# Rearranging the first prologue of a four-layer transformer kernel on one Trainium2 core

## The chip, the cores and the metric

The kernel is one program on one core of one Trainium2 chip. The metric is the device time of one execution in microseconds (us). A core has five engines that run side by side, each with its own instruction stream: TensorE (PE: matrix products and transposes), VectorE (DVE), ScalarE (ACT), GpSimd (POOL) and SyncE (SP), which here only issues DMAs. ACT and POOL can issue DMAs too. Engines wait for one another through semaphores. A wait stands in an engine's stream, so everything behind it on that engine waits as well.

## The reference

Four residual layers work on `x` of 8 batches x 256 tokens x 512 channels: a rotary cross-attention, a mixture of experts, a second cross-attention, and a layer of routed weight maps. Cut to what this case touches, the first attention and the part of the last layer that is prepared beside it:

```python
# first layer, per batch: 32 heads of 16 channels
q = rope((layernorm(x) @ Wq)); k, v = split(ctx @ Wkv); k = rope(k)
w = softmax(einsum('bqhd,bkhd->bhqk', q, k) / 4)
x = x + tanh(g_xattn[0]) * (einsum('bhqk,bkhd->bqhd', w, v) @ Wout + bout)
...
# last layer: 4096 values added to a 512 x 512 map, for each of 8 experts
deltas = softmax(expert_atom_weights) @ atoms          # (8, 4096)
weighted = deltas * sigmoid(importance)
rows, cols = mask_idx // 512, mask_idx % 512
out = xt @ W.T + segment_sum((xt[:, cols] * vals).T, rows).T
```

The kernel builds the last layer's maps ahead of time: a `table` in DRAM has one row of eight values (one for each expert) for each entry of the 512 x 512 map. It is filled with `W` eight times side by side, and then the 4096 weighted values are added to its rows.

## The kernel before

`rope_attention` is the first stage. It takes about 616 of the 2049.5 us. Its work is cut into slots `s`, from -21 to 132. Each engine's block is a loop over the slots, and tables of numbers (`FIRST_ITEMS_AT`, `WIDEN_AT`, `SEND_AT`, `ROWS_AT`, `FIRST_COLUMN_AT`, ...) say what an engine puts into a slot. So the order on each engine is written out by hand. Slots 0 to 127 hold one pair of heads each (16 pairs for each of 8 batches). The negative slots are the first prologue: batch 0's projections and transposes, with nothing to overlap them with.

A pair `g` runs through this chain. PE computes its scores (`scores(g)`, L1142, in slot g - 2) into two PSUM banks `a_SC`. DVE takes the maxima (`top`, L844). ACT takes the exponentials (L962). PE turns them back (`turn_exponentials`, L1153). There is one pair of score banks, so `scores(g + 1)` waits for the exponentials of `g`. Every fourth slot has the product with V (`weighted`, L1168 and L1175). It needs `a_recw`, a copy of the reciprocal denominators that POOL writes two slots earlier (`widened`, L659).

Beside this chain the stage does four other things that the change touches:

- The units (`q0a`, `k1b`, ...) are transposed pieces of q and k: PE turns them (L1057), then ACT copies the ones of token half 0 and DVE those of half 1 (L994, L884) out of the three PSUM banks `a_W`. The next item on a bank waits for that copy. `scores(0)` needs the units q0a, q1a, k0a, k1a, and `exchange`: eight DMAs (L539, 64 KB each) that copy `qT` to `qS` with halves swapped, once for each half `a` and `b` of the heads. Here SP issues all of them.
- The widening: eight times ACT copies a part of `W` eight-fold into one of five buffers (`widen`, L1010, tiles `st_wide`), and SP sends 1 MB of it to `table` (`send_wide`, L584). Buffers 2, 3 and 4 are used twice, so the second widening into a buffer waits until the first one's transfer has landed. It uses ACT ahead of ACT's unit copies.
- The weighted values: PE multiplies atoms and expert weights (items `E0`, `E1`: 64 small matmuls, L1106), and DVE makes three bf16 parts of the result (`place_weights`, L769 to L784). Later slots compare indices (`match`), sum equal ones (`S0`, `S1`), and POOL adds 32 columns of sums to the table with indirect DMAs (`add_column`, L692). Each addition waits until the one before it has landed (`scattered`), and the first for `placed`.
- The expert weights are loaded in pieces, split by POOL into a high and a low part (L671, L673), and stored again by SP (L551, L559, L561).

```python
for s in range(FIRST, LAST):           # SP's block, L615 to L627
    for b, n in items(s):
        if n[0:2] == "q1":
            exchange(b, "ab".index(n[-1]))
    late_loads(s)                      # send_wide, x, row indices, Wout
```

## Time and profile before

| | |
|---|---|
| median of 3 runs | 2059.47 us (2052.32 to 2062.51) |
| profiled execution | 2051.53 us, span of its records 2049.5 us |
| PE / DVE / ACT / POOL busy | 89% / 57% / 45% / 47% of the span |
| mean granted TensorE clock | 0.948 of full speed |
| DMA, mean over the span | 202 GB/s |

The profile is that of one execution. A row of its timeline gives the start (us from the span's start), the time from the start of the first to the end of the last instruction that it merges, the engine, the line, the operation with what it writes and reads, the count, and in brackets how long the engine had been idle before it and what released it. The prologue is short: `scores(0)` starts at 59.8 us. In it PE is busy about half of the time; from about 155 us to the stage's end it is nearly always busy.

### The profile page before, as it was taken

What the parts mean: (1) busy time and instruction counts of PE and PEld (TensorE: products, weight loads), DVE (VectorE), ACT (ScalarE), POOL (GpSimd) and SP (SyncE); (2) the same over time, 40 slices, a digit from 0 to 9 for tenths busy, and PEclk for the clock granted to TensorE, in tenths of its full rate; (3) what the DMA queues carried; (4) which work ended last, traced back from release to release, by engine and by line L of the source; (5) the groups of instructions that cost most, each with busy time, mean ns of one, the idle gap of its engine ahead of it and who ended that gap; (6) DMA issues with size and microseconds to landing.
All of it is one profiled execution on the core that took longest, in us unless ns stands there. A gap on an engine that the chain in (4) does not pass through costs nothing. (4 is left out here: it accounts for less than half of the span.)

```text
span 2049.5 us, 38711 instructions
## 1 busy us (share of the span) xinstructions
PE 1829.9 (89%) x11488; PEld 1407.2 (69%) x11488; DVE 1177.7 (57%) x2665; ACT 924.0 (45%) x2630; POOL 962.0 (47%) x1018
## 2 busy tenths in 40 slices
PE   4779999999987999999999999994789999786992
PEld 2546666565656999999999999992455566555881
DVE  5766776776654875333333353325777778764445
ACT  5456766776752332233333333321466666640110
POOL 2368876887751354133343333422455555212560
PEclk9789999999998999999999999997899999996996
DMA  8777887778767246488998987533344545539647
GB/s 266 246 216 217 272 250 225 242 253 268 238 205 264 79 146 196 152 243 269 332 332 254 271 270 199 106 70 109 89 109 104 119 99 119 127 108 360 234 164 275
DMA packets 234892, 414.81 MB, mean 202 GB/s; under 512 B 44313, under 2 KB 121409, under 8 KB 228938
## 3 DMA queue, kind: packets, MB, share of 16 engines
q1 hardware_dynamic: 168330, 324.12, 49.5%
q0 software_dynamic: 30592, 62.54, 13.0%
q10 hardware_dynamic: 35776, 25.69, 4.0%
q8 instruction: 106, 1.74, 0.3%
q14 instruction: 88, 0.72, 0.1%
HBM read 211.97 MB, written 157.82 MB: 180 GB/s over the span
## 5 line engine op out<-in xcount | busy, mean ns | idle before, releaser
L962 ACT ACTIVATE a_P<-a_SC,a_nm 128x256 f32<-128x256 f32 x512 | 235.5, 472 | 142.2 <-DVE a_nm L844 141.5
L1538 POOL DMA_INDIRECT b_y_rows<-b_ysb,b_entry x79 | 124.4, 1574 | 335.4 <-ACT b_ysb L1686 188.7
L844 DVE TENSOR_REDUCE a_nm<-a_SC 128x2 f32<-128x512 f32 x256 | 164.6, 685 | 127.9 <-PE a_SC L1142 127.8
L673 POOL TENSOR_TENSOR a_praw<-a_praw,a_phigh 128x704 f32<-128x704 f32 (+2 forms) x126 | 191.7, 1522 | 10.3
L1790 DVE TENSOR_TENSOR b_xl<-b_XT,b_xh 128x512 fp32r<-128x512 f32 x97 | 67.0, 691 | 214.2 <-ACT b_xh L1692 213.8
L1153 PEld LDWEIGHTS a_T<-ident,a_P 128*128 128x128 f32 x1024 | 119.1, 144 | 83.4 <-issue 43.7
L1153 PE MATMUL a_T<-ident,a_P 128*128 128x128 f32 x1024 | 147.5, 283 | 26.0 <-DVE a_PT L856 24.1
L671 POOL CAST a_phigh<-a_praw 128x704 fp32r<-128x704 f32 (+2 forms) x126 | 111.0, 881 | 106.5 <-DMA a_praw<-in_L_ffn_wd 29.3
L1796 DVE TENSOR_TENSOR b_al<-b_AT,b_ah 128x384 fp32r<-128x384 f32 x111 | 61.8, 557 | 153.0 <-ACT b_ah L1697 153.0
L2524 ACT ACTIVATE c_P<-c_SC,c_nm 128x240 f32<-128x240 f32 x256 | 115.5, 456 | 75.6 <-DVE c_P L2395 75.6
L1686 ACT ACTIVATE b_ysb<-b_Y 128x512 f32<-128x512 f32 x79 | 47.2, 597 | 221.7 <-PE b_Y L1633 215.7
L1697 ACT ACTIVATE b_ah<-b_AT 128x384 fp32r<-128x384 f32 x111 | 54.6, 492 | 199.9 <-PE b_AT L1622 199.9
L1517 POOL DMA_INDIRECT b_slots<-b_ysb,b_at_u x64 | 65.4, 1021 | 104.5 <-DVEq L1883 86.2
L962 ACT ACTIVATION_READ_ACCUMULATOR a_P<-a_SC,a_nm 128x1 f32 x512 | 103.9, 203 | 0.0
L1525 POOL DMA_INDIRECT b_xg<-b_xn_rows,b_entry x79 | 78.4, 993 | 53.2 <-issue 22.2
L2389 DVE TENSOR_REDUCE c_nm<-c_SC 128x2 f32<-128x480 f32 x128 | 81.9, 640 | 36.3 <-PE c_SC L2699 35.8
L1633 PE MATMUL b_Y<-b_wh,b_ah 128*128 (+1 forms) x333 | 95.8, 396 | 0.9 <-ACT b_ah L1697 0.9
L1633 PE MATMUL b_Y<-b_wh,b_al 128*128 (+1 forms) x333 | 94.5, 392 | 0.0
L2709 PE MATMUL c_T<-ident,c_P 128*128 128x128 f32 x512 | 71.4, 280 | 25.9 <-POOL c_P L2316 16.8
L1633 PE MATMUL b_Y<-b_wl,b_ah 128*128 (+1 forms) x333 | 94.3, 391 | 0.0
L1142 PE MATMUL a_SC<-a_kT,a_qT 32*128 32x256 f32 x512 | 81.7, 332 | 13.5 <-ACT a_P L962 6.2
L2709 PEld LDWEIGHTS c_T<-ident,c_P 128*128 128x128 f32 x512 | 57.3, 142 | 52.9 <-POOL c_P L2316 25.3
(495 smaller groups left out, 4907.8 us busy)
## 6 DMA issues: line engine op xcount, KB each, us to landing
w_parts<-a_phigh SPq DMA_DIRECT2D x72, 352.0 KB, 3.7
w_parts<-a_praw SPq DMA_DIRECT2D x72, 352.0 KB, 4.1
b_wh<-w_parts SPq DMA_DIRECT2D x18, 1216.0 KB, 10.0
b_wl<-w_parts SPq DMA_DIRECT2D x18, 1216.0 KB, 13.8
c_q<-c_qT SPq DMA_DIRECT2D x64, 256.0 KB, 4.0
c_k<-c_kT SPq DMA_DIRECT2D x124, 128.0 KB
b_wh<-w_parts SPq DMA_DIRECT2D x18, 704.0 KB, 4.7
b_wl<-w_parts SPq DMA_DIRECT2D x18, 704.0 KB, 7.3
```

What stands on the lines that cost most here:

```text
L671: eng.tensor_copy(high[:, 0:k * m], raw[:, 0:k * m]).then_inc(phigh_done, 1)
L673: eng.tensor_tensor(raw[:, 0:k * m], raw[:, 0:k * m], r32(high[:, 0:k * m]), ALU.subtract).then_inc(plow_done, 1)
L844: eng.tensor_reduce(nm[:, g % 4, j, :], SC[j][:, :].rearrange("p (t k) -> p t k", t=BT), AX.X, ALU.max, negate=True).then_inc(topped, 1)
L962: e = eng.activation(Pr[:, i, t, :], SC[j][:, t * S:(t + 1) * S], ACT.Exp, bias=nm[:, g % 4, j, t:t + 1], accum_out=den[:, h, t:t + 1])
L1142: m = eng.matmul(SC[j][:, t * S:(t + 1) * S], q[r:r + R, p // 2, t * P:(t + 1) * P], kT[r:r + R, p // 2, :], start=(half == 0), stop=(half ...
L1153: m = eng.transpose(T_[j][:, k * S + t * P:k * S + (t + 1) * P], Pr[:, (2 * g + j) % NP_, t, k * P:(k + 1) * P], core.ident[:, :])
L1525: eng.indirect_dma_start(out=xg[:, row(v), :], out_offset=None, in_=xn_rows, in_offset=bass.IndirectOffsetOnAxis(ap=entry[:, r, 1:2].bitca ...
L1538: eng.indirect_dma_start(out=y_rows, out_offset=bass.IndirectOffsetOnAxis(ap=entry[:, r, 1:2].bitcast(U32), axis=0), in_=ysb[:, v % RING, ...
L1633: m = eng.matmul(Y[v % 2][:, :], a_[:, v % 2, j * P:(j + 1) * P], down_rows(w_, at_unit[v], j), start=(i == 0), stop=(i == 3 * J - 1))
L2389: eng.tensor_reduce(nm[:, g % 4, j, :, 0], v[:, :, 0:MAIN], AX.X, ALU.max, negate=True)
L2524: e = eng.activation(Pr[:, i, t, 0:MAIN], SC[j][:, t * S:t * S + MAIN], ACT.Exp, bias=nm[:, g % 4, j, t, 0:1], accum_out=den[:, h, t, 0:1])
L2709: m = eng.transpose(T[j][:, k * S + t * P:k * S + (t + 1) * P], Pr[:, (2 * g + j) % NP_, t, k * P:(k + 1) * P], core.ident[:, :])
```

## The change

Six edits, all in `rope_attention`:

1. The items `E0`, `E1` move from slot -4 to slot -1, so the units k1a and k1b come one slot earlier, and `E` comes behind `scores(0)`. `place_weights` moves on DVE from slot -3 to slot 1, behind the units, the second layer norm (`second_stats`, from slot -6 to -2) and the first maxima.
2. The widenings 6 and 7 move from slots -7 and -5 to -5 and -4, behind ACT's copies of q0b and k0b, and their sends from SP's -4 to -3. The sends of 4 and 5 come one slot earlier, so the send of 4 stands ahead of the first exchange on SP.
3. The first exchange is cut in two: SP issues four of its DMAs and ACT the other four, behind its last V copy.
4. ACT computes one exponential of 8 values at the end of its prologue, so the table of `Exp` is loaded there.
5. The 32 table additions are issued in slots 15 + 7i//2 (15, 18, 22, 25, 29, 32, ..., 123) and no longer in 13, 14, 15, 17 and then every fourth slot from 19 to 127.
6. `Wout` is loaded in four parts of 256 KB in slots 14 to 17, and no longer in one of 1 MB in slot 14. The first load of row indices comes a slot later.

```diff
-                      ... -5: ("q1b",), -4: ("E0", "E1"), -3: ("k1a",), -2: ("k1b",), ...
+                      ... -5: ("q1b",), -4: ("k1a",), -3: ("k1b",), -1: ("E0", "E1"), ...
-    COLUMN_AT = {3: 0, 7: 1, 11: 2, 15: 3}
-    FIRST_COLUMN_AT = {13: 0, 14: 1, 15: 2, 17: 3}
+    COLUMN_FROM = 15
-    WIDEN_AT = {-14: (1, 2), -13: (3,), -12: (4,), -9: (5,), -7: (6,), -5: (7,)}
-    SEND_AT = {-12: (0, 1), -10: (2, 3), -8: (4,), -6: (5,), -4: (6, 7)}
+    WIDEN_AT = {-14: (1, 2), -13: (3,), -12: (4,), -9: (5,), -5: (6,), -4: (7,)}
+    SEND_AT = {-12: (0, 1), -10: (2, 3), -9: (4,), -7: (5,), -3: (6, 7)}
-    ROWS_AT = {-1: 0, 3: 1, 5: 2, 8: 3}
+    ROWS_AT = {0: 0, 3: 1, 5: 2, 8: 3}
@@ sync
-                if s == 14:
+                if 14 <= s < 14 + KD:
                     eng.wait_ge(placed, 1)
-                    eng.dma_start(wo[:, :, :], kview(Wout)).then_inc(wo_in, 16)
+                    eng.dma_start(wo[:, s - 14, :], kview(Wout)[:, s - 14, :]).then_inc(wo_in, 16)
-                        exchange(b, "ab".index(n[-1]))
+                        exchange(eng, b, "ab".index(n[-1]), range(0, P // 2 if (b, n) == (0, "q1a") else P, HD))
@@ gpsimd
-                for b, n in due(s, FIRST_COLUMN_AT, COLUMN_AT):
-                    add_column(4 * b + n)
+                for i in range(C):
+                    if s == COLUMN_FROM + 7 * i // 2:
+                        add_column(i)
@@ vector
-                if s == -3:
+                if s == 1:
                     place_weights()
-                if s == -6:
+                if s == -2:
                     second_stats()
@@ scalar
+                if s == -7:
+                    exchange(eng, 0, 0, range(P // 2, P, HD))
                 if s == -3:
                     eng.wait_ge(graw_in, 32)
                     eng.activation(core.gates[:, :], graw[:, :], ACT.Tanh).then_inc(gates_set, 1)
+                    eng.wait_ge(ea_scaled, 4)
+                    eng.activation(s1[:, :], m1[:, :], ACT.Exp)
                     eng.wait_ge(wide_ready, 8)
@@ tensor
-                    eng.wait_ge(wo_in, 16)
+                    eng.wait_ge(wo_in, 16 * KD)
```

Three places show how the instructions move. The first is ACT's stream in the prologue, from widening 5 (tile `st_wide_63`) on; `st_wide_64` is widening 6 and `st_wide_62` widening 7. Before:

```order
L1010 ACTIVATE st_wide_63<-st_Wraw 128x2048 [waits a_wide_out3,a_W_in]
L1001 ACTIVATE a_V<-a_W 128x16x2x16 [waits a_consts,a_W_filled]
L1010 ACTIVATE st_wide_64<-st_Wraw 128x2048 [waits a_wide_out4,a_W_in]
L994 ACTIVATE a_qT<-a_W 128x4x128 [waits a_W_filled]
L994 ACTIVATE a_kT<-a_W 128x4x128 [waits a_W_filled]
L1010 ACTIVATE st_wide_62<-st_Wraw 128x2048 [waits a_wide_out2,a_W_in]
```

After:

```order
L1011 ACTIVATE st_wide_63<-st_Wraw 128x2048 [waits a_wide_out3,a_W_in]
L1002 ACTIVATE a_V<-a_W 128x16x2x16 [waits a_consts,a_W_filled]
L530 DMA a_qS<-a_qT 16x1024 [waits a_W_free0,a_W_free2]
L530 DMA a_qS<-a_qT 16x1024 x3
L995 ACTIVATE a_qT<-a_W 128x4x128 [waits a_W_filled]
L995 ACTIVATE a_kT<-a_W 128x4x128 [waits a_W_filled]
L1011 ACTIVATE st_wide_64<-st_Wraw 128x2048 [waits a_wide_out4,a_W_in]
L1011 ACTIVATE st_wide_62<-st_Wraw 128x2048 [waits a_wide_out2,a_W_in]
```

The unit copies of q0b and k0b no longer stand behind a widening that waits for a transfer (`a_wide_out4`), but behind four DMA issues that wait for the copies of q0a and q1a.

The second is PE's stream from the transposes of q1b on (`a_hlq` is q, `a_hlk` is k). Before:

```order
L1057 MATMUL a_W<-ident,a_hlq 128x128 x3
L1106 MATMUL a_W<-a_eaT,st_atoms 128x8 [waits a_eaT_set,a_atoms_in,a_W_free0,a_W_free2]
L1106 MATMUL a_W<-a_eaT,st_atoms 128x8 x31
L1057 MATMUL a_W<-ident,a_hlk 128x128 [waits a_W_free1,a_lo_done]
L1057 MATMUL a_W<-ident,a_hlk 128x128 x3
L1057 MATMUL a_W<-ident,a_hlk 128x128 [waits a_W_free2,a_lo_done]
L1057 MATMUL a_W<-ident,a_hlk 128x128 x3
L1142 MATMUL a_SC<-a_kT,a_qT 128x256 [waits a_W_free1,a_swapped0,a_W_free0,a_W_free2]
```

After:

```order
L1062 MATMUL a_W<-ident,a_hlq 128x128 x3
L1062 MATMUL a_W<-ident,a_hlk 128x128 [waits a_W_free2,a_lo_done]
L1062 MATMUL a_W<-ident,a_hlk 128x128 x3
L1062 MATMUL a_W<-ident,a_hlk 128x128 [waits a_W_free0,a_lo_done]
L1062 MATMUL a_W<-ident,a_hlk 128x128 x3
L1147 MATMUL a_SC<-a_kT,a_qT 128x256 [waits a_W_free2,a_W_free1,a_swapped0,a_W_free0]
L1147 MATMUL a_SC<-a_kT,a_qT 128x256
L1147 MATMUL a_SC<-a_kT,a_qS 128x256 x2
L1147 MATMUL a_SC<-a_kT,a_qT 128x256 x2
L1147 MATMUL a_SC<-a_kT,a_qS 128x256 x2
L1111 MATMUL a_W<-a_eaT,st_atoms 128x8 [waits a_eaT_set,a_atoms_in,a_W_free2,a_W_free1]
L1111 MATMUL a_W<-a_eaT,st_atoms 128x8 x31
```

The `E` matmuls stood ahead of the k1 units; now they stand between the first and the second scores.

The third is POOL's stream in slots 13 to 15, from the piece of slot 13 on (L671 and L673 are a piece, L692 an addition, L659 the copy for `weighted(3)`). Before:

```order
L673 TENSOR_TENSOR a_praw<-a_praw,a_phigh 128x512 [waits a_phigh_done]
L692 DMA table<-a_place_sums,a_place_rows 266240x8 [waits a_wide_out2,a_wide_out1,a_wide_out3,a_wide_out0,a_wide_out4,a_zeros_out,a_placed]
L671 CAST a_phigh<-a_praw 128x512 [waits a_phigh_out0,a_praw_in0]
L673 TENSOR_TENSOR a_praw<-a_praw,a_phigh 128x512 [waits a_phigh_done]
L692 DMA table<-a_place_sums,a_place_rows 266240x8 [waits a_scattered]
L671 CAST a_phigh<-a_praw 96x512 [waits a_phigh_out1,a_praw_in1]
L673 TENSOR_TENSOR a_praw<-a_praw,a_phigh 96x512 [waits a_phigh_done]
L659 COPY a_recw<-a_rec 128x256 [waits a_weighted_done,a_rec_done]
L692 DMA table<-a_place_sums,a_place_rows 266240x8 [waits a_scattered]
```

After:

```order
L673 TENSOR_TENSOR a_praw<-a_praw,a_phigh 128x512 [waits a_phigh_done]
L671 CAST a_phigh<-a_praw 128x512 [waits a_phigh_out0,a_praw_in0]
L673 TENSOR_TENSOR a_praw<-a_praw,a_phigh 128x512 [waits a_phigh_done]
L671 CAST a_phigh<-a_praw 96x512 [waits a_phigh_out1,a_praw_in1]
L673 TENSOR_TENSOR a_praw<-a_praw,a_phigh 96x512 [waits a_phigh_done]
L659 COPY a_recw<-a_rec 128x256 [waits a_weighted_done,a_rec_done]
L692 DMA table<-a_place_sums,a_place_rows 266240x8 [waits a_wide_out2,a_wide_out1,a_wide_out3,a_wide_out0,a_wide_out4,a_zeros_out,a_placed]
```

Two additions stood ahead of the copy; now none does, and the first one follows it.

## Rows read from the trace of the kernel before

**Rows 1.** Windows: length; busy of PE, PEld, DVE, ACT, POOL; clock; DMA share; GB/s.

```profile
35.00:40.00 5.00, 3.08 (x16) 1.74 (x14) 4.48 (x22) 1.75 (x2) 0.00 (x0) 1.00 0.41 65
...
50.00:55.00 5.00, 5.00 (x50) 5.00 (x50) 0.00 (x0) 1.22 (x2) 0.00 (x0) 0.50 1.03 373
```

**Rows 2.** Windows again: a later stretch of the same stage.

```profile
155.00:185.00 30.00, 29.48 (x219) 18.64 (x221) 23.15 (x48) 21.40 (x76) 27.23 (x24) 0.99 0.79 254
```

**Rows 3.** Timeline of ACT, prologue: start us, length us, what, idle before.

```profile
36.70 0.60 ACT L1001 ACTIVATE a_V<-a_W 128x512 f32<-128x512 f32 x1 [0.56 <-PE a_W L1067]
46.45 1.91 ACT L1010 ACTIVATE st_wide<-st_Wraw 128x2048 f32<-128x2048 f32 x1 [9.14 <-DMA table<-st_wide]
...
61.78 1.28 ACT L962 ACT_TABLE_LOAD   x1 [10.56 <-DVE a_nm L844]
```

**Rows 4.** Timeline of PE, prologue.

```profile
49.43 7.00 PE L1106 MATMUL a_W<-a_eaT,st_atoms 64*128 64x8 f32 x64 [11.35 <-ACT a_qT L994]
...
59.79 0.58 PE L1142 MATMUL a_SC<-a_kT,a_qT 32*128 32x256 f32 x2 [1.47 <-DVE a_kT L884]
```

**Rows 5.** Timeline of SP's DMA issues, the first exchange.

```profile
35.77 5.02 SPq L539 DMA_DIRECT2D a_qS<-a_qT  x8
```

**Rows 6.** Timeline of DVE, prologue.

```profile
35.59 1.28 DVE L109 BATCH_NORM_STATS2 st<-X 128x6 f32<-128x512 f32 x2
...
40.45 0.69 DVE L884 CAST a_qT<-a_W 128x512 fp32r<-128x512 f32 x1
56.47 0.48 DVE L769 TENSOR_TENSOR st_wgt<-st_imp,a_W 128x128 f32<-128x128 f32 x2 [15.33 <-PE a_W L1106]
...
58.64 0.29 DVE L780 CAST a_parts<-st_rest 128x256 bf16<-128x256 f32 x1
...
61.01 1.29 DVE L844 TENSOR_REDUCE a_nm<-a_SC 128x2 f32<-128x512 f32 x2 [0.88 <-PE a_SC L1142]
66.37 1.29 DVE L844 TENSOR_REDUCE a_nm<-a_SC 128x2 f32<-128x512 f32 x2 [4.07 <-PE a_SC L1142]
...
70.50 1.29 DVE L844 TENSOR_REDUCE a_nm<-a_SC 128x2 f32<-128x512 f32 x2 [1.58 <-PE a_SC L1142]
```

**Rows 7.** Tile `a_qS`, 0 to 200 us: from issue to landing.

```profile
DMA to landing us min/median/max: 2.2/2.3/3.7
```

**Rows 8.** Tile `X`, 0 to 160 us: the same, transfers queued behind others.

```profile
DMA to landing us min/median/max: 3.9/9.8/12.6
```

**Rows 9.** DMA issues on ACT, second stage: ns of one issue, min/median/max.

```profile
L1710 ACTq DMA_DIRECT2D b_mraw<-table x16: 407/748/6194, 619.7 to 1297.1; - x16
```

**Rows 10.** Timeline of PE, `weighted` of slot 13 and of slot 17.

```profile
129.75 0.44 PE L1168 MATMUL a_O<-ident,a_recw 128*128 128x128 f32 x2
...
133.00 0.39 PE L1142 MATMUL a_SC<-a_kT,a_qT 32*128 32x256 f32 x2
...
144.33 0.66 PE L1057 MATMUL a_W<-ident,a_xn 128*128 128x128 f32 x4
149.39 0.66 PE L1168 MATMUL a_O<-ident,a_recw 128*128 128x128 f32 x2 [4.40 <-issue]
...
155.45 0.38 PE L1142 MATMUL a_SC<-a_kT,a_qT 32*128 32x256 f32 x2
```

**Rows 11.** Timeline of POOL, slots 14 and 15.

```profile
145.39 1.59 POOL L692 DMA_INDIRECT table<-a_place_sums,a_place_rows  x1 [4.59 <-DMA table<-a_place_sums,a_place_rows]
...
148.90 0.39 POOL L659 COPY a_recw<-a_rec 128x256 f32<-128x256 f32 x1
```

**Rows 12.** Timeline of SP: load of the 96x512 piece that POOL splits in slot 15.

```profile
137.70 0.34 SPq L551 DMA_DIRECT2D a_praw<-in_L_ffn_sd  x1
```

**Rows 13.** Tile `a_praw`, 0 to 200 us: from issue to landing.

```profile
DMA to landing us min/median/max: 2.5/4.2/7.6
```

**Rows 14.** Timeline of POOL: a later copy for `weighted`.

```profile
364.51 0.42 POOL L659 COPY a_recw<-a_rec 128x256 f32<-128x256 f32 x1
```

**Rows 15.** Timeline of PE: the use of that copy.

```profile
366.94 0.38 PE L1168 MATMUL a_O<-ident,a_recw 128*128 128x128 f32 x2
```

18 lines of the change are left out of this document (9 added, 9 removed).

## The prediction

> **What bounds the kernel now.** I read the windows first. Once the stage runs, PE is busy for 29.48 of 30 us [rows 2], so a microsecond that the prologue loses or wins is passed on whole: no other engine sets the pace there (POOL, next, is busy for 27.23). In the prologue it is otherwise: PE works 3.08 of 5 us, and the DMA engines are busy for 0.41 of the time [rows 1]. So the time is in waits, and the timelines say which.
>
> The longest chain runs through ACT. Its V copy ends at 37.30, and then it stands for 9.14 us at a widening that waits for a table transfer [rows 3]. That transfer stood on SP behind the exchange, which takes SP from 35.77 to 40.79 [rows 5]. The unit copies of q0b and k0b stand behind the widening on ACT, and PE waits 11.35 us for the first of them, until 49.43, because `E` needs its bank [rows 4]. Then come `E` (7.00 us), the k1 units, and the first scores at 59.79 [rows 4]. PE's clock is meanwhile at half, 1.2 GHz (1.00 before, 0.50 now) [rows 1]. DVE idles 15.33 us for `E` [rows 6]. The row that I measure the prologue by is the third maxima, at 70.50 [rows 6]; from there on both kernels do the same.
>
> There is a second hole: PE idles 4.40 us before `weighted(3)` [rows 10], because POOL stood 4.59 us at an addition that waits for the one before it, and wrote the copy that PE needs only at 148.90 [rows 11].
>
> **The prologue, part by part.** I write the new times forward from 37.30, where nothing has changed yet.
>
> ACT's four DMA issues. SP's eight took 5.02 us, 0.63 each [rows 5]; ACT's own issues later have a median of 0.75 and a maximum of 6.19 [rows 9]. I take 0.7, near both, so 2.8 us: ACT is free at 40.1. Its two unit copies cost 0.6 each, as the V copy [rows 3], and end at 41.3. PE turns k1b in 0.66 (the same four transposes as at 144.33 [rows 10]), to 42.0, and DVE copies it in 0.69 [rows 6], to 42.7. No widening stands here any more: its transfer is now sent ahead of the exchange, and widenings 6 and 7 run behind the unit copies, where ACT has 1.9 us for each [rows 3] until the maxima at 47.6 (below): 41.3 + 3.8 = 45.1, covered by 2.5 us.
>
> The exchange. The last of ACT's four is issued at 40.1. Exchanges landed after 2.2 to 3.7 us [rows 7]; transfers queued behind others after up to 12.6 [rows 8]. Here a 1 MB table transfer and 3 MB of `x` are issued at the same time on SP's queue. I take 3.7, the upper end of the same kind of transfer: 43.8. For the range it is 42.3 to 52.7. The Trainium skill ("DMA: Bandwidth & Descriptors", "Issuing engines are not separate DMA queues") says that issuing from several engines saves only issue time, since all share the same 16 DMA engines. By that rule the cut of the exchange is worth 2.2 us of issuing (5.02 less 2.8) and no transfer time, and since it puts 2.8 us in front of ACT's unit copies it is close to nothing; the sum above gives it no more. The same page ("Queues, rings and completion order") says that a DMA engine takes turns between queues packet by packet; by it the landing is near 3.7, not 12.6.
>
> Scores(0) run from 43.8 for 1.2 us (59.79 to 61.01 [rows 4, 6]), to 45.0. DVE meanwhile does the second layer norm, now behind k1b: 35.59 to 40.45 before, at most 4.9 us [rows 6], so to 47.6. The maxima and exponentials of pair 0 follow; from the maxima to the next scores took 4.1 us with the table load (61.01 to 65.2, which is 66.37 less 1.2 for the scores [rows 6]), 2.9 without its 1.28 [rows 3]. So they are done at 50.5. But PE is in `E` from 45.0, at half clock 7.00 us, to 52.0. So `E` decides, and the layer norm and the table load are both hidden behind it: I count the loading of the table early as nothing. Will the clock be at half? Before, it fell after PE had stopped at 38.08 for 11.35 us [rows 4]; now PE works 1.3 of the 5.7 us before the scores, on the k1 units. I take the low clock. At 2.4 GHz `E` would take 3.5, and then the exponentials decide, at 50.5.
>
> Scores(1) end at 53.2. The maxima of pair 1, the reciprocals and two statistics last 2.55 (66.37 to 68.92, which is 70.50 less 1.58 idle [rows 6]): 55.8. Now `place_weights` stands here, 56.47 to 58.93, 2.46 us [rows 6]. It had stood in front of `scores(0)` and partly beside transposes; here it delays the third maxima by what it exceeds their wait: they would be ready 4.1 us after the second (66.37 to 70.50 [rows 6]), at 57.3, and start at 58.2. So it costs 0.9 here.
>
> Third maxima at 58.2 against 70.50: **12.3 us won**. With a fast `E` 56.7 (13.8 won); with the exchange landing at 52.7, 67.1 (3.4 won); if all four issues took 6.19 [rows 9], ACT would be free at 62.1, the exchange landed at 65.8 and the maxima came at 80.2 (9.7 lost).
>
> **The additions and `Wout`.** PE is ready for `weighted(3)` at 144.33 + 0.66 = 144.99. At full clock it takes 3.25 us from there to the next scores (129.75 to 133.00); it came to them at 155.45 [rows 10]. So 155.45 - 144.99 - 3.25 = 7.2 us are to be won, the idle time and the slow clock behind it. (All these times shift together by the 12.3.) Does POOL come in time? Its piece is loaded at 137.70 [rows 12] and lands 4.2 later at the median [rows 13], at 141.9. From the addition to the copy it took 3.51, of it 1.59 the addition [rows 11], so 1.9 for the piece and 0.4 for the copy: 144.2, early by 0.8. With a landing of 7.6 it is late by 2.6, and 4.6 are won. The additions cost as much as before (32 issues of 1.6); two now stand between the copies of slots 15 and 19, and POOL has little room there [rows 2], and SP has three more issues for `Wout` at 0.4 or so. For both I take 1.0 off, an estimate. Net **6.2**. `Wout` itself is needed in slot 28, ten slots behind its last part. The row indices have until slot 2: nothing.
>
> **Sum.** 12.3 + 6.2 = 18.5. The profiled execution took 2051.53 (2049.5 of span and 2.0 around it), so it would take 2033.0. The median of the three runs, 2059.47, is 7.9 above that execution. Taken from it: 2041.0.
>
> **Rivals.**
>
> *The exchange lands late or ACT issues slowly.* For it: 4 MB go out beside it, and such transfers took up to 12.6 us [rows 8]. Against it: exchanges never took over 3.7 [rows 7], and they go on a queue of their own, for which the rule on taking turns stands above. Then 3.4 + 6.2 = 9.6: 2050.
>
> *The second hole comes back.* POOL still waits for pieces from SP, whose loads stand behind exchanges; a landing near 7.6 [rows 13] in slot 15 or 19, with the clock falling again, eats most of the 7.2. Then some 12.3 + 1: 2046.
>
> *Nothing arrives.* The stage would have to end by something with its own clock, such as pieces or the table. Against it: PE is full there and the pieces are bound to slots. 2058.
>
> *Slower: the denser additions make PE wait again and again.* Before, each four-slot stretch from slot 19 on had one addition. Now those of slots 16 to 19, 44 to 47, 72 to 75 and 100 to 103 have two. POOL's copy was done at 364.93 and used at 366.94: 2.0 us of room [rows 14, 15]. An addition takes 1.59 [rows 11], which fits; the point from which it decides is 2.0, that is, when the addition must also wait for the one before, as at 145.39. Then each costs what it cost there, 7.2: four cost 28.8, and 2041.0 + 28.8 = 2070. Against it: three slots are some 10 us at least (3.25 for the work of a part of one [rows 10]), longer than the landings of rows 7 and 13.
>
> **Chances.** The forecast 0.60, with a range of its own from 2033 to 2047; late exchange 0.13; the second hole 0.13; nothing 0.08; slower 0.06. A measurement of this kernel can tell about 0.5%, 10.3 us, from no change: faster is below 2049.2. Forecast and second hole lie below it, the late exchange at it, split 0.05 to 0.08. So faster 0.78, same 0.16, slower 0.06. The range: the low end takes the fast `E` (1.5 more), and runs that lie as far below their median as the quickest of before (7.2), so some 2030; the high end has the late exchange and some of the case without effect: 2056.
>
> **What would show it.** Widening 6 no longer waits (9.14 us gone); PE's 11.35 us before `E` gone; `scores(0)` near 44, `E` behind it near 45 with 7 us at clock 0.5; third maxima near 58; `place_weights` between second and third maxima; no idle time before L1168 at about 133, and clock 1.00 there; rows of the later stages shifted by about 18. Wrong would be: first scores behind 50, DVE's layer norm or ACT's issues found as what PE waits for, or L1168 waiting again.

## The result and the profile after

| | before | changed |
|---|---|---|
| median of 20 runs each | 2055.39 us (2051.72 to 2064.85) | 2043.5 us (2039.22 to 2056.1) |
| profiled execution, and its span | 2051.53, 2049.5 us | 2045.0, 2043.3 us |
| mean granted TensorE clock | 0.948 | 0.947 |

The ratio is 0.9948, 95% interval 0.9936 to 0.996: 10.7 us faster (8.2 to 13.2). Forecast were 2041.0 us and 18.5 us of gain. (The interval is for the means; the medians are 11.9 us apart.) So the level was met within 2.5 us, but the gain was forecast 7.8 us too large. Part of the difference is the starting point: the median of before over 20 runs is 4.1 us below that of the three runs from which I took the gain off.

First the prologue, the timeline of ACT in the changed kernel (columns as in [rows 3]):

```profile
36.69 0.60 ACT L1002 ACTIVATE a_V<-a_W 128x512 f32<-128x512 f32 x1 [0.55 <-PE a_W L1072]
36.75 2.52 ACTq L530 DMA_DIRECT2D a_qS<-a_qT  x4
39.32 0.60 ACT L995 ACTIVATE a_qT<-a_W 128x512 fp32r<-128x512 f32 x1 [2.03 <-issue]
39.81 0.59 ACT L995 ACTIVATE a_kT<-a_W 128x512 fp32r<-128x512 f32 x1
40.29 3.71 ACT L1011 ACTIVATE st_wide<-st_Wraw 128x2048 f32<-128x2048 f32 x2
...
44.11 1.28 ACT L1049 ACT_TABLE_LOAD   x1
...
47.58 0.47 ACT L963 ACTIVATE a_P<-a_SC,a_nm 128x256 f32<-128x256 f32 x1 [1.97 <-DVE a_nm L845]
```

The 9.14 us of idle time before a widening [rows 3] are gone. Four DMA issues take 2.52 us, the unit copies follow at once, and the two widenings and the table load are done before ACT has to wait for the first maxima. PE in the same stretch:

```profile
40.06 1.12 PE L1062 MATMUL a_W<-ident,a_hlk 128*128 128x128 f32 x8 [2.00 <-ACT a_qT L995]
44.62 0.58 PE L1147 MATMUL a_SC<-a_kT,a_qT 32*128 32x256 f32 x2 [3.44 <-DMA a_qS<-a_qT]
...
45.77 7.00 PE L1111 MATMUL a_W<-a_eaT,st_atoms 64*128 64x8 f32 x64
52.70 0.58 PE L1147 MATMUL a_SC<-a_kT,a_qT 32*128 32x256 f32 x2
```

Of the 11.35 us of [rows 4], two waits are left, 2.00 and 3.44 us. The windows show that PE's clock is at half (1.2 GHz) here, and stays there for 10 us in which PE never stops (columns as in [rows 1]). Before them PE had stood for 2.00 and 3.44 us:

```profile
45.00:50.00 5.00, 5.00 (x48) 4.78 (x48) 2.65 (x12) 2.53 (x10) 1.53 (x2) 0.50 1.05 395
50.00:55.00 5.00, 5.00 (x40) 4.75 (x41) 1.05 (x2) 0.33 (x1) 0.00 (x0) 0.50 1.07 258
```

DVE's maxima, the rows by which I measure:

```profile
53.95 1.29 DVE L845 TENSOR_REDUCE a_nm<-a_SC 128x2 f32<-128x512 f32 x2 [5.87 <-PE a_SC L1147]
...
56.41 0.47 DVE L770 TENSOR_TENSOR st_wgt<-st_imp,a_W 128x128 f32<-128x128 f32 x2
...
58.77 1.28 DVE L845 TENSOR_REDUCE a_nm<-a_SC 128x2 f32<-128x512 f32 x2
...
66.13 3.06 DVE L795 TENSOR_TENSOR st_eq<-st_row_i,a_idx_i 128x512 bf16<-128x512 int32 x2
69.19 1.29 DVE L845 TENSOR_REDUCE a_nm<-a_SC 128x2 f32<-128x512 f32 x2
```

The third maxima come at 58.77 against 70.50 [rows 6]: 11.7 us won. Two pairs further on the lead is 9.4. The comparison of indices in front of the fifth maxima takes 3.06 us for two instructions; in the kernel before the same two took 1.27. The tile's row has the longer of the two (ns, min/median/max):

```profile
L795 DVE TENSOR_TENSOR st_eq<-st_row_i,a_idx_i x2: 969/1566/2162, 66.1 to 67.0; 128x512 bf16<-128x512 int32 x2
```

One execution of spacing_alone and one of e_halves (the profiled one) took over 3300 us at a low clock; they are left out below. Now the second hole. POOL in slots 15 and 16:

```profile
136.27 0.40 POOL L659 COPY a_recw<-a_rec 128x256 f32<-128x256 f32 x1
136.84 1.79 POOL L692 DMA_INDIRECT table<-a_place_sums,a_place_rows  x1 [0.17 <-issue]
...
146.33 0.77 POOL L671 CAST a_phigh<-a_praw 128x704 fp32r<-128x704 f32 x1 [5.13 <-DMA a_praw<-in_L_ffn_wg]
...
157.12 0.39 POOL L659 COPY a_recw<-a_rec 128x256 f32<-128x256 f32 x1
```

And PE, at `weighted(3)` and `weighted(4)`:

```profile
139.02 0.38 PE L1173 MATMUL a_O<-ident,a_recw 128*128 128x128 f32 x2
...
157.87 0.66 PE L1173 MATMUL a_O<-ident,a_recw 128*128 128x128 f32 x2 [2.60 <-POOL a_recw L659]
```

The 4.40 us at `weighted(3)` [rows 10] are gone, since no addition stands in front of its copy. But one `weighted` later PE waits 2.60 us for the next copy, and runs at the low clock behind it (its matmuls take 2.99 us, where those of `weighted(3)` took 1.93 at full clock):

```profile
158.00:160.00 2.00, 2.00 (x18) 0.92 (x22) 0.62 (x1) 2.00 (x9) 1.92 (x3) 0.50 0.76 236
```

POOL waited 5.13 us for a piece. SP's timeline tells when that piece was loaded, and behind what:

```profile
132.56 0.38 SPq L551 DMA_DIRECT2D a_praw<-in_L_ffn_wg  x1
134.14 4.94 SPq L530 DMA_DIRECT2D a_qS<-a_qT  x8
139.13 0.58 SPq L612 DMA_DIRECT2D a_wo<-in_L_xattn_Wout  x1
139.75 1.47 SPq L559 DMA_DIRECT2D w_parts<-a_phigh  x1
141.27 0.43 SPq L561 DMA_DIRECT2D w_parts<-a_praw  x1
141.75 0.46 SPq L551 DMA_DIRECT2D a_praw<-in_L_ffn_wg  x1
```

Between two loads of pieces lie 9.2 us. They hold an exchange of batch 1 (eight issues, 4.94 us), one part of `Wout`, and two stores.

### The profile page after: what moved, and what is told of

Same layout as the page of the kernel before. It is cut to its first block and busy times, and to the rows that moved or that the text cites. A ratio compares the mean times of both kernels' runs of the same rounds, so it can differ in the third digit from the quotient of the medians.

```text
span 2043.3 us, 38716 instructions
## 1 busy us (share of the span) xinstructions
PE 1836.0 (90%) x11488; PEld 1411.4 (69%) x11488; DVE 1181.0 (58%) x2665; ACT 925.6 (45%) x2631; POOL 961.7 (47%) x1018
## 3 DMA queue, kind: packets, MB, share of 16 engines
q0 software_dynamic: 30592, 62.54, 13.2%
## 5 line engine op out<-in xcount | busy, mean ns | idle before, releaser
L673 POOL TENSOR_TENSOR a_praw<-a_praw,a_phigh 128x704 f32<-128x704 f32 (+2 forms) x126 | 193.8, 1538 | 10.3
L671 POOL CAST a_phigh<-a_praw 128x704 fp32r<-128x704 f32 (+2 forms) x126 | 106.5, 845 | 107.1 <-DMA a_praw<-in_L_ffn_wd 33.4
L1530 POOL DMA_INDIRECT b_xg<-b_xn_rows,b_entry x79 | 78.3, 991 | 53.2 <-issue 22.5
```

The source lines that it names most:

```text
L671: eng.tensor_copy(high[:, 0:k * m], raw[:, 0:k * m]).then_inc(phigh_done, 1)
L673: eng.tensor_tensor(raw[:, 0:k * m], raw[:, 0:k * m], r32(high[:, 0:k * m]), ALU.subtract).then_inc(plow_done, 1)
L1530: eng.indirect_dma_start(out=xg[:, row(v), :], out_offset=None, in_=xn_rows, in_offset=bass.IndirectOffsetOnAxis(ap=entry[:, r, 1:2].bitca ...
```

## The experiments

Each ran beside the kernel before. The runs fall in four groups, each on a chip of its own, and I compare kernels with those of their own group. A difference of medians stands with a 95% interval for the difference of means (n = 5 to 11), worked out from the single times. The kernel before had medians of 2056.3, 2058.1, 2060.7 and 2056.3 us in the four groups (1: wout_one and wout_late; 2: spacing_alone, spacing_undone, wout_single, e_halves; 3: pieces_first, rows_early, whole_on_sp, four_together; 4: three_together, e_interleaved).

Only group 1 has a repeat of the changed kernel. In group 2 wout_single stands in for it, and in group 3 rows_early. That these two are worth nothing of their own rests on their profiles and on times within 1 us of the changed kernel's on other chips. Against the kernel before of their own group they gain 17.3 and 16.5 us, where the changed kernel and its repeat gain 10.7 and 11.9, so times of different groups can't settle it.

The starts of `weighted(n)` in each profile tell where time is won and lost (us from the timelines of PE; in brackets the idle time before it):

| | 0 | 2 | 3 | 4 | 5 | 9 | 31 |
|---|---|---|---|---|---|---|---|
| before | 87.52 | 129.75 | 149.39 (4.40) | 168.33 | 183.70 | 249.73 | 609.79 |
| changed | 78.22 | 122.30 | 139.02 | 157.87 (2.60) | 175.27 | 240.82 | 602.60 |
| wout_one (a repeat) | 77.99 | 120.30 | 135.37 | 156.38 (4.76) | 175.51 | 240.87 | 600.96 |
| spacing_alone | 89.46 | 133.22 | 149.93 | 168.44 (2.26) | 185.78 | 251.83 | 615.07 |
| spacing_undone | 76.95 | 121.36 | 139.51 (2.91) | 157.81 | 173.43 | 241.17 | 601.63 |
| wout_single | 78.18 | 120.43 | 135.50 | 155.29 (3.54) | 175.60 | 241.31 | 604.44 |
| wout_late | 77.27 | 121.32 | 136.40 | 154.31 (1.67) | 169.72 | 235.99 | 595.82 |
| pieces_first | 79.09 | 121.45 | 138.10 | 156.13 (1.77) | 171.52 | 237.19 | 595.89 |
| rows_early | 76.57 | 120.93 | 136.02 | 156.12 (3.85) | 176.40 | 241.17 | 601.55 |
| four_together | 79.80 | 122.15 | 137.23 | 153.32 | 168.70 | 234.42 | 591.58 |
| three_together | 78.00 | 120.34 | 136.49 | 152.59 | 168.20 | 233.89 | 589.68 |
| e_interleaved | 75.06 | 120.80 | 135.87 | 151.95 | 167.33 | 233.11 | 590.84 |

Each line is one profile, and some of its differences are no effect of an edit. Both kernels have other holes ahead of `weighted(2)`, which the prediction left out. There PE waits for a copy that DVE makes, while DVE is busy with a layer norm for later batches. First the longest one in the kernel before, then one of the changed kernel:

```profile
108.10 1.09 PE L1153 MATMUL a_T<-ident,a_P 128*128 128x128 f32 x4 [3.11 <-DVE a_PT L856]
```

```profile
106.13 1.09 PE L1158 MATMUL a_T<-ident,a_P 128*128 128x128 f32 x4 [2.44 <-DVE a_PT L857]
```

Every profile in the table has one or two holes of this kind, of 1.9 to 3.1 us, between 90 and 120 us, and the low clock there for some 7 to 15 us in all. No edit was aimed at them. By `weighted(2)` two profiles of kernels that do the same up to there differ by up to 3.5 us, so I also count from `weighted(2)`.

**spacing_alone: the kernel before with the additions' spacing only.**

```diff
-    COLUMN_AT = {3: 0, 7: 1, 11: 2, 15: 3}
-    FIRST_COLUMN_AT = {13: 0, 14: 1, 15: 2, 17: 3}
+    COLUMN_FROM = 15
...
-                for b, n in due(s, FIRST_COLUMN_AT, COLUMN_AT):
-                    add_column(4 * b + n)
+                for i in range(C):
+                    if s == COLUMN_FROM + 7 * i // 2:
+                        add_column(i)
```

> The kernel before with one part of the change: the table additions start at slot 15 and come 3.5 slots apart (32 of them, as before). Prologue and Wout as before. Theory A (the sum's 7.2 us for the second hole is right): L1173's idle time of 4.40 us before weighted(3) goes and its scores follow at full clock. In the two runs that have this spacing with the new prologue a hole of 1.7 to 4.8 us stood before weighted(4) instead; by theory A it is caused by the new neighbours (earlier prologue, Wout in four) and is not here: 6 to 8 us faster than before, 2048. Theory B (spacing 3.5 slots puts a second addition in front of the copy of slot 19 whatever else is done): idle time at weighted(4) here too, 3 us faster than before or less, 2053.

2054.1 us, ratio to before 0.9977 (0.996 to 0.9994): 4.7 us faster (1.2 to 8.2). The profile is nearer to theory B. The idle time at `weighted(3)` is gone, 2.26 us stand before `weighted(4)` with the low clock behind them, and POOL waits 2.54 and 2.74 us for two pieces there. Counted from `weighted(2)`, which comes 3.5 us later here than in the profile of before, 3.4 us are won by `weighted(4)` and 1.4 by `weighted(5)` (52.56 us in place of 53.95), of the 7.2 that theory A had. So the holes are no two independent losses. How much of the 4.7 us comes from here this one profile can't tell: the stage's last `weighted` comes 5.3 us later in it than before.

**spacing_undone: the changed kernel without the spacing.**

```diff
-    COLUMN_FROM = 15
+    COLUMN_AT = {3: 0, 7: 1, 11: 2, 15: 3}
+    FIRST_COLUMN_AT = {13: 0, 14: 1, 15: 2, 17: 3}
...
-                for i in range(C):
-                    if s == COLUMN_FROM + 7 * i // 2:
-                        add_column(i)
+                for b, n in due(s, FIRST_COLUMN_AT, COLUMN_AT):
+                    add_column(4 * b + n)
```

> The changed kernel with the additions where they stood before (slots 13, 14, 15, 17, then four in each block of 32), all else changed. Theory A: it has the prologue's gain alone. The third maxima stay at 58.8; POOL waits again 4 to 5 us at the addition of slot 15, PE idles again some 4 us before weighted(3), and no hole stands before weighted(4). About 3 us slower than the changed kernel (7.2 lost, 4.1 won back): 2046.5. Theory B (the hole at weighted(4) comes from pieces that land late and not from the additions): both holes are there, and it is 7 us or more slower, 2051.

2044.6 us; against wout_single of the same group +0.8 in the medians (means -4.5 to 3.4). The hole is back at `weighted(3)` (2.91 us, with POOL at an addition for 2.71), and none is at `weighted(4)`, which starts at 157.81. In the changed kernel it starts at 157.87, in its repeat at 156.38. Theory A had the places right; its price of 3 us is not seen, but lies inside the interval. From `weighted(2)` to `weighted(5)` the kernel takes 52.07 us without the spacing and 52.97 and 55.21 with it. With the new prologue too, the spacing moves the hole by one `weighted` and wins nothing that these profiles show.

**wout_one, and wout_single: how `Wout` is loaded.** The kernel that ran as wout_one is not the one that its text speaks of: it still loads `Wout` in four, and only PE's wait asks for the first part alone, in slot 28, where all have long landed. So it is a repeat of the changed kernel. wout_single is what was meant:

```diff
-                if 14 <= s < 14 + KD:
+                if s == 14:
                     eng.wait_ge(placed, 1)
-                    eng.dma_start(wo[:, s - 14, :], kview(Wout)[:, s - 14, :]).then_inc(wo_in, 16)
+                    eng.dma_start(wo[:, :, :], kview(Wout)).then_inc(wo_in, 16)
...
-                    eng.wait_ge(wo_in, 16 * KD)
+                    eng.wait_ge(wo_in, 16)
```

> The changed kernel with Wout loaded as before in one DMA at slot 14 in place of four at slots 14 to 17. Theory A (the hole before weighted(4), 2.60 us of idle time and a slow clock, comes from SP's three extra issues, behind which the loads of pieces stand): the piece that landed 5.13 us late at POOL's 146.33 comes 1 to 2 us earlier, and 2 to 4 us are won: 2040 to 2041.5. Theory B (it comes from the 1 MB of Wout itself, or from the two additions between slots 15 and 19): the hole stays within 1 us, possibly earlier by a slot, and the time is within 1.5 us of the changed kernel.

The repeat: 2043.3 us. Its idle time before `weighted(4)` is 4.76 us where the first profile had 2.60, so the hole varies by 2 us between two profiles of one kernel.

> The changed kernel with Wout loaded as before in one DMA at slot 14 in place of four at slots 14 to 17. With the four loads put in slots 20 to 23 it was 4.5 us faster, POOL's wait for the piece 3.72 in place of 5.13, PE's idle time before weighted(4) 1.67 in place of 2.60 (4.76 in a repeat of the changed kernel), and the clock did not fall. Theory A (SP's issues are it: 0.5 to 0.6 us for each of the three more): 1 to 2 us of the wait go, and it is 2 to 4.5 us faster than the changed kernel. Theory B (the 1 MB of Wout beside the pieces is it, in whatever number of loads): within 1.5 us of the changed kernel, since the same bytes go out at slot 14.

2043.9 us, 3.54 us of idle time before `weighted(4)`, and the low clock behind it. That is theory B's side: with three issues fewer on SP the hole is as it was, within what it varies by. The time can't settle it, since no run of the changed kernel stands in this group. The three more issues were one of the two reasons for which I had taken 1.0 us off, and the profile shows no cost of them.

**wout_late: the four loads in slots 20 to 23.**

```diff
-                if 14 <= s < 14 + KD:
+                if 20 <= s < 20 + KD:
                     eng.wait_ge(placed, 1)
-                    eng.dma_start(wo[:, s - 14, :], kview(Wout)[:, s - 14, :]).then_inc(wo_in, 16)
+                    eng.dma_start(wo[:, s - 20, :], kview(Wout)[:, s - 20, :]).then_inc(wo_in, 16)
```

> The changed kernel with the four parts of Wout loaded in slots 20 to 23 in place of 14 to 17; they are needed in slot 28. Theory A (Wout's transfers or their issues delay the pieces of slots 16 to 18): POOL's wait of 5.13 us for the piece goes down to 1 to 2, the copy for weighted(4) comes 3 us earlier, PE's 2.60 us of idle time is gone: 3 to 4 us faster than the changed kernel, about 2040. Theory B (two additions between the copies of slots 15 and 19 are it): the hole stays and the time is within 1.5 us of the changed kernel. If the hole moves to where the loads now stand, the time is the same also, but the idle time stands at weighted(5) or later.

2038.9 us, 4.5 less than the repeat of the same group (1.5 to 8.8). Its POOL and PE:

```profile
143.01 0.77 POOL L671 CAST a_phigh<-a_praw 128x704 fp32r<-128x704 f32 x1 [3.72 <-DMA a_praw<-in_L_ffn_wg]
```

```profile
154.31 0.41 PE L1173 MATMUL a_O<-ident,a_recw 128*128 128x128 f32 x2 [1.67 <-POOL a_recw L659]
```

The idle time is down to 1.67 us, and the clock does not fall: from `weighted(4)` to `weighted(5)` it takes 15.4 us here and 17.4 in the changed kernel, 19.1 in the repeat. So the megabyte beside the pieces counts, by wout_single the number of its issues doesn't, and the clock behind the hole costs about as much as the hole: 3.1 us less than the repeat up to `weighted(4)`, 3.7 less from there to `weighted(5)`. POOL's wait went down by 1.4 us and not to 1 to 2: something else holds the piece.

**pieces_first: SP loads pieces before it issues an exchange (from batch 1 on).**

```diff
                 for b, n in items(s):
-                    if n[0:2] == "q1":
+                    if b == 0 and n[0:2] == "q1":
                         exchange(...)
                 late_loads(s)
                 ...
                     load_piece(i)
+                for b, n in items(s):
+                    if b and n[0:2] == "q1":
+                        exchange(...)
```

> The changed kernel with SP's order turned in each slot from batch 1 on: the slot's pieces are stored and loaded first, and the eight issues of an exchange (4.94 us on SP) come behind them. What the spacing was to win at weighted(3) came back as a hole at weighted(4), with the additions respaced and with them where they were. Theory A (POOL's wait of 5.13 us at slot 16 is for a piece whose load stands behind the exchange on SP, issued at 134.14 to 139.08): the load is issued some 5 us earlier, POOL's wait falls below 1, the copy for weighted(4) is early, no idle time before weighted(4) and no low clock there: 3 to 5 us faster than the changed kernel, and the same order may save a little at later exchanges. Theory B (the pieces are late because their bytes are many: 352 KB each way beside Wout, at any place in the queue): the wait keeps 4 us or more, within 1 us. Rival C: the exchange now lands too late for the first scores of its half batch, and PE waits there: slower by 1 us or more at each of 15 exchanges.

2040.7 us, 3.7 less than rows_early of the same group (0.4 to 7.7), which has the other order on SP and the edit that is told below. POOL and SP:

```profile
138.39 0.77 POOL L674 CAST a_phigh<-a_praw 128x704 fp32r<-128x704 f32 x1 [0.34 <-DMA a_praw<-in_L_ffn_wg]
...
147.36 0.77 POOL L674 CAST a_phigh<-a_praw 128x704 fp32r<-128x704 f32 x1 [6.42 <-DMA a_praw<-in_L_ffn_wu]
```

```profile
133.10 0.38 SPq L551 DMA_DIRECT2D a_praw<-in_L_ffn_wg  x1
133.59 4.97 SPq L530 DMA_DIRECT2D a_qS<-a_qT  x8
138.61 1.42 SPq L612 DMA_DIRECT2D a_wo<-in_L_xattn_Wout  x1
```

The piece that was late by 5.13 us is late by 0.34. The next one, which now stands behind the exchange, is late by 6.42 (its slot has more time). What reaches PE is 1.77 us, with no fall of the clock. That the exchange comes too late (rival C) shows nowhere: PE never waits for `a_qS` behind the first one. So the exchange on SP and `Wout` each make a part of the hole: without the one 1.77 us are left, without the other 1.67, of 2.60 and 4.76.

**rows_early: the first row indices in a buffer of their own, loaded in slot -4.**

```diff
-    ROWS_AT = {0: 0, 3: 1, 5: 2, 8: 3}
+    ROWS_AT = {-4: 0, 3: 1, 5: 2, 8: 3}
...
+        row_first = lies("row_first", [P, ROWS, P], I32, nc.sbuf_base - 4 * 2 * BT * S)
...
-                    else:
-                        filled(eng, (0, "E1"))
```

> The changed kernel with the first row indices in a place of their own (the end of PT, free until slot 5), loaded in slot -4; they no longer wait for E. Theory A (DVE's comparison at 66.13 lasts 3.06 instead of the 1.27 of before because it waits 1.8 us for the indices, and the fifth and sixth maxima are late by that): the comparison takes 1.3, the fifth maxima come at 67.4 in place of 69.19, and 1.8 us stay won: 2041.7. Theory B (at slot 2 PE, with its clock at half and Q's products of 3.78 us, decides): the comparison is short, but the maxima at 69 and later stay, and the time is within 1 us.

2044.4 us, as the changed kernel on another chip. The fifth maxima come at 67.55, near theory A's 67.4, but its cause was wrong: in the changed kernel the load was issued at 53.22 and landed after 11.5 us, at 64.7, before DVE came to the comparison. And two pairs on, the next comparisons take 2.40 us where the changed kernel has 1.28, and 0.5 us of the lead is left. The two timelines of DVE and POOL, first in rows_early:

```profile
65.77 1.85 DVE L794 TENSOR_TENSOR st_eq<-st_row_first,a_idx_i 128x512 bf16<-128x512 int32 x2
67.55 1.27 DVE L844 TENSOR_REDUCE a_nm<-a_SC 128x2 f32<-128x512 f32 x2
...
76.70 2.40 DVE L794 TENSOR_TENSOR st_eq<-st_row_i,a_idx_i 128x512 bf16<-128x512 int32 x2
```

```profile
65.89 1.19 POOL L670 CAST a_phigh<-a_praw 128x704 fp32r<-128x704 f32 x1 [17.82 <-DMA a_praw<-in_L_ffn_sg]
67.16 1.99 POOL L672 TENSOR_TENSOR a_praw<-a_praw,a_phigh 128x704 f32<-128x704 f32 x1
```

and in e_interleaved (below), where DVE comes to it 3.4 us before POOL has its first piece:

```profile
63.13 1.27 DVE L797 TENSOR_TENSOR st_eq<-st_row_first,a_idx_i 128x512 bf16<-128x512 int32 x2
...
75.19 3.81 DVE L797 TENSOR_TENSOR st_eq<-st_row_i,a_idx_i 128x512 bf16<-128x512 int32 x2
```

```profile
66.52 0.77 POOL L673 CAST a_phigh<-a_praw 128x704 fp32r<-128x704 f32 x1 [18.11 <-DMA a_praw<-in_L_ffn_sg]
67.37 1.69 POOL L675 TENSOR_TENSOR a_praw<-a_praw,a_phigh 128x704 f32<-128x704 f32 x1
```

Alone, two comparisons take 1.27 us, POOL's cast 0.77 and its subtraction 1.69. Where they overlap, the first two comparisons take 1.85 (rows_early) to 3.22 us (three_together, whose indices are early as well), POOL's cast up to 1.19 and its subtraction 1.99 to 2.00. In e_interleaved the first two are free of POOL, and the next two, beside POOL's second piece, take 3.81. It is contention between DVE and POOL, which an earlier DVE moves to other instructions. The Trainium skill ("SBUF — State Buffer", "SBUF: two separate sides") says that the two share a pair of ports as an exclusive lock: a VectorE operation with two SBUF inputs and a GpSimd operation that reads SBUF don't run beside each other, and the later one waits. The traces agree in that instructions which touch nothing of each other get longer by up to the length of the other (one comparison 2.16 us in place of 0.68 beside a subtraction of 1.99).

**whole_on_sp: the first exchange issued by SP alone.**

```diff
-    exchange(eng, b, "ab".index(n[-1]), range(0, P // 2 if (b, n) == (0, "q1a") else P, HD))
+    exchange(eng, b, "ab".index(n[-1]), range(0, P, HD))
...
-                if s == -7:
-                    exchange(eng, 0, 0, range(P // 2, P, HD))
```

> The changed kernel with the first exchange issued by SP alone, eight DMAs as before, none by ACT. Theory A (the sum: two queues save issue time, 2.2 us of it, but put 2.8 us in front of ACT's unit copies): SP issues from 35.8 to 40.8, the exchange lands 2.2 to 3.7 later, at 43.0 to 44.5 as now (44.6), the k1 units come 2.5 us earlier on ACT, and the time is within 1 us of the changed kernel. Theory B (the cut on two queues is worth its 2.2 us): scores(0) come 2 us later, E and all behind them too, 2 us slower. The third maxima tell: 58.8 by A, 61 by B.

2046.2 us, 1.8 more than rows_early (-2.2 to 5.6): not to be told from none. In its profile the load of `W` landed 4.0 us later than in the changed kernel, in a stretch that the edit does not touch, and all behind is 4 to 6 us late, so absolute times don't compare. From the first issue of the exchange to `scores(0)` they do:

```profile
41.81 5.02 SPq L530 DMA_DIRECT2D a_qS<-a_qT  x8
```

```profile
48.79 0.39 PE L1145 MATMUL a_SC<-a_kT,a_qT 32*128 32x256 f32 x2 [3.68 <-DMA a_qS<-a_qT]
```

That is 7.0 us on one queue; on two it is 8.9 (35.76 to 44.62), and 8.8 to 9.0 in the seven other profiles that have this cut and all of `E` behind `scores(0)`. After the last issue it took 2.0 us on one queue, and 5.3 on two (39.27 to 44.62). With the exchange cut, SP sends 1 MB of table and three parts of `x` beside ACT's half. The 2.5 us of issue time saved were more than paid back by the landing: edit 3 made `scores(0)` wait some 1.9 us longer, an estimate from these profiles, which the times neither show nor exclude.

**e_halves: `E0` before `scores(0)`, `E1` behind.**

```diff
-                      -3: ("k1b",), -1: ("E0", "E1"), ...
+                      -3: ("k1b",), -2: ("E0",), -1: ("E1",), ...
...
-                        for h in range(2):
+                        for h in (int(n[1]),):
```

> The changed kernel with E in two halves of 16 products: E0 before scores(0), E1 behind them (both stood behind them). Theory A (E decides when scores(1) come, and PE is idle for 3.44 us before scores(0)): E0 (3.5 us at the low clock) runs from 40.7 to 44.2 in that idle time, scores(0) stay at 44.6, E1 ends at 49.3, scores(1) wait for the exponentials of pair 0 and come at 50.5 to 51 in place of 52.70; DVE, which would then decide, gives the third maxima at 57 in place of 58.77: 1.5 to 2.2 us faster in the prologue, and the clock may come back sooner than 69, up to 2 us more. Theory B (DVE's work and the row indices decide behind scores(1)): scores(1) come earlier, and by the fifth maxima nothing is left of it. Rival C: the order makes PE wait for a bank or for atoms and scores(0) come late: slower by the 3.5 us.

2044.7 us, 0.8 more than wout_single (-2.8 to 4.9). No profile of it is read here; the next run shows what the cut did.

**four_together: pieces_first, wout_late, rows_early and e_halves in one.**

> The changed kernel with four edits at once: pieces before exchanges on SP, Wout in slots 20 to 23, the first row indices early in a place of their own, and E in two halves around scores(0). Theory A (each takes away a different wait: hole before weighted(4) 3 to 5 us, indices 1.8, E 1.5 to 2.2): 6 to 9 us faster than the changed kernel, 2035 to 2037, and the first version that beats both kernels by more than the difference between runs. Theory B (from weighted(0) on the first stage is paced by POOL with the pieces, which are bound to slots and to DMA, so that what the prologue wins is given back by weighted(4)): no more than wout_late gave, 2039.

2040.4 us, 0.2 less than pieces_first (5.7 less to 4.4 more), so a smaller gain than theory A had. PE:

```profile
40.89 5.88 PE L1113 MATMUL a_W<-a_eaT,st_atoms 64*128 64x8 f32 x32
...
47.85 6.99 PE L1113 MATMUL a_W<-a_eaT,st_atoms 64*128 64x8 f32 x32
```

The second half of `E` takes as long as the whole of it: 32 instructions in 6.99 us, where 64 took 7.00, both at clock 0.50. (The first half, 5.88 us, began at a higher clock: 0.79 from 41 to 43 us, 0.50 behind.) So the second maxima come at 56.02, 2.1 us later than in the changed kernel. But no idle time is left before `weighted(4)`.

**three_together and e_interleaved: the three edits without the cut, and with the other cut.** Here the parts of `E` are the first and the second half of the columns, each with both row halves in turn:

```diff
-                      -3: ("k1b",), -1: ("E0", "E1"), ...
+                      -3: ("k1b",), -2: (("E0", 0, 1), ("E1", 0, 1)), -1: (("E0", 1, 2), ("E1", 1, 2)), ...
...
-                    for i in range(CH):
+                    for i in range(CH // 2 * i0, CH // 2 * i1):
                         for h in range(2):
```

> The changed kernel with three edits: pieces before exchanges on SP, Wout in slots 20 to 23, the first row indices early; E whole, in one stretch behind scores(0). In four_together the halves of E took 5.88 and 6.99 us, 12.87 in all where the whole took 7.00, and the second maxima came at 56.02 in place of 53.95. Theory A (halving E cost 2 us of the prologue, the other three edits keep the hole at weighted(4) closed): second maxima at 53.9, no idle time before weighted(4), which stands at 151 to 152 (153.32 in four_together), 1 to 2 us faster than four_together: 2038 to 2039.5 beside a kernel before at 2059. Theory B (POOL's wait for pieces paces the first 150 us, whenever the prologue ends): weighted(4) at 153 to 154 again, some idle time before it, and the same time as four_together within 1 us.

2034.7 us, ratio to before 0.9891 (0.9872 to 0.991). `weighted(4)` starts at 152.59 without idle time; that is theory A's side (it had 151 to 152, and 2038 to 2039.5 us).

> As three_together, but E cut the other way: each part has 16 products of both row halves in turn (32 matmul instructions at 109 ns), one part before scores(0), one behind. Theory A (the products of rows 0 to 63 and of rows 64 to 127 run beside each other when they alternate, as 64 in 7.00 us against 32 in 6.99 suggest): each part takes 3.5 us at the low clock, the first lies in PE's idle time before scores(0), scores(1) come at 50.5 to 51 in place of 52.7 and the third maxima at 57 in place of 58.8: 1.5 us faster than three_together. Theory B (the cost was in cutting E, whatever the cut): the parts take 6 to 7 us each as in four_together and it is 2 us slower than three_together. If the parts take 3.5 us and the time is the same, DVE and POOL decide behind it.

2032.4 us, ratio to before 0.9877 (0.9858 to 0.9896), 2.3 less than three_together (5.5 less to 0.4 more). PE and DVE:

```profile
41.51 3.59 PE L1113 MATMUL a_W<-a_eaT,st_atoms 64*128 64x8 f32 x32 [0.34 <-issue]
45.03 0.58 PE L1149 MATMUL a_SC<-a_kT,a_qT 32*128 32x256 f32 x2
...
46.18 3.58 PE L1113 MATMUL a_W<-a_eaT,st_atoms 64*128 64x8 f32 x32
49.70 0.58 PE L1149 MATMUL a_SC<-a_kT,a_qT 32*128 32x256 f32 x2
```

```profile
50.95 1.29 DVE L847 TENSOR_REDUCE a_nm<-a_SC 128x2 f32<-128x512 f32 x2 [2.87 <-PE a_SC L1149]
...
55.77 1.28 DVE L847 TENSOR_REDUCE a_nm<-a_SC 128x2 f32<-128x512 f32 x2
```

Theory A's mechanism holds: 3.6 us for each part at clock 0.50, and the third maxima come 2.8 us earlier than in three_together (58.54). Its 1.5 us in the time are not told apart from none. By `weighted(4)` 0.6 of the 2.8 is left in the two profiles, and at the end of the span 1.2 (2030.7 and 2031.9). This is the version that beats both kernels: its slowest run (2033.92) lies below the fastest of the changed kernel (2039.22, on another chip).

## Why the prediction was right, and where it was not

*Prologue, 12.3 us forecast, 11.7 found: right, step by step.* ACT free at 40.1 (39.3 found), unit copies done at 41.3 (40.4), exchange landed at 43.8 (44.6), `E` from 45.0 for 7.00 at half clock (45.77, 7.00), second maxima at 53.2 (53.95), third at 58.2 (58.77), with `place_weights` in front of them as expected. That `E` decides, with the layer norm and the table load hidden behind it, is confirmed from the other side by e_interleaved: with `E` cut well the third maxima come 2.8 us earlier and nothing else had to move. The early table load was not tried by itself. The landing was mis-sized (3.7 us forecast, 5.3 found, nearer to it than to the 12.6 of the range), which was partly offset by ACT's issues (2.52 us in place of 2.8) and copies. By the rule of the Trainium skill ("DMA: Bandwidth & Descriptors", "Issuing engines are not separate DMA queues") I gave the cut of the exchange no more than its issue time. The traces agree that it saves no more (2.5 us), and show a price that I had at nothing: the landing is 3.3 us longer after the last issue.

*"From there on both kernels do the same": wrong.* The lead shrinks from 11.7 to 9.4 us by the fifth maxima. What I had left out is that a prologue 11.7 us shorter meets pieces that land only 3 us earlier (POOL's first cast at 65.78 against 68.89). So DVE's comparisons now fall on POOL's first piece and take 1.8 us longer, most of the 2.3. I had taken the row indices as worth nothing, and their load is: it landed in time. For the same reason "all these times shift together by the 12.3" failed: PE was ready for `weighted(3)` at 139.02 in place of 144.99, 6.0 us earlier, and 9.6 in the repeat.

*The second hole, 6.2 us forecast: this step failed.* "So 155.45 - 144.99 - 3.25 = 7.2 us are to be won", less 1.0. The first half was right: at `weighted(3)` neither idle time nor low clock is left. The 1.0 for what comes back was mis-sized (us between starts):

| | before | changed | repeat |
|---|---|---|---|
| `weighted(2)` to `weighted(3)` | 19.64 | 16.72 | 15.07 |
| `weighted(3)` to `weighted(4)` | 18.94 | 18.85 | 21.01 |
| `weighted(4)` to `weighted(5)` | 15.37 | 17.40 | 19.13 |
| sum | 53.95 | 52.97 | 55.21 |

So between `weighted(2)` and `weighted(5)` 1.0 us was won in the first profile and 1.3 lost in the repeat, in place of 6.2. It is what the rival "the second hole comes back" had, at its own price (12.3 + 1), and in its way: POOL waits for a piece whose load stands behind an exchange on SP. I had given it 0.13, because I had only asked whether POOL is in time for slot 15 (it was: 136.27 against 139.02) and left slot 19 to an estimate. One reason for that estimate was no change at all: two additions stood between the copies of slots 15 and 19 before, too (150.85 and 157.59). spacing_alone and spacing_undone show that it is no chance of one run: with either prologue the hole before a `weighted` stands at `weighted(3)` with the old spacing and at `weighted(4)` with the new. What removes it is time for the pieces. pieces_first and wout_late each take away a part. In the three runs that have both no idle time is left; all three load the row indices early as well, and none has the two edits alone.

*The sum.* In the profiled pair 11.7 - 2.3 - 1.9 + 1.0 = 8.5 us are won by `weighted(5)` (183.70 less 175.27 is 8.4; the repeat has 8.2). The 1.9 were lost between the fifth maxima and `weighted(2)`, where PE's clock fell twice in this profile, behind the holes in which it waits for DVE, and the repeat lost none of them. Both values lie in the interval of the 10.7 us measured (8.2 to 13.2). The rest, up to 2.5 us, these profiles don't place: the executions of one kernel lie 13 to 17 us apart, and the pair that was profiled is 6.5 apart where the medians are 11.9. That the forecast met the time within 2.5 us is in part luck: the gain was overestimated by 6.6 us in the medians, and the three runs had put the start 4.1 too high.

*Slower by double additions:* shown nowhere. The first of its four places, slots 16 to 19, is where the hole now stands, but there it is the late piece that POOL waits for and not an addition (no addition waits for the one before it), and no `weighted` from 5 on has idle time before it.

## What to carry to other kernels

Idle time that two waits share is won only once both are gone. Before an edit takes away the wait that ends last, write down for the next two or three uses of the same engine which wait ends second, and what it costs. Here the row to read was the load on SP behind eight exchange issues, besides the addition on POOL. On a queue that serves several customers, put first what an engine will stand for soonest, and spread bulk loads with slack (`Wout`) to where no other transfer is urgent. And when a stage comes earlier, ask which of its instructions will now overlap others that did not move with it.
